# Writing out the loop over pairs of heads in a two-layer cross-attention kernel

## The reference, cut to what matters

```python
# layer 0: 8 heads of 16; layer 1: 16 heads of 32, with layer norms ahead of its projections
Qh, Kh, Vh = split(Q @ W_q), split(K @ W_k), split(V @ W_v)
scores = jnp.einsum('bqhd,bkhd->bhqk', Qh, Kh) * scale      # 4096 x 3202 for each head
attn = jax.nn.softmax(scores, axis=-1)
ctx = jnp.einsum('bhqk,bkhd->bqhd', attn, Vh).reshape(b, lq, H * DV)
X = Q + ctx @ W_o
...
# layer 0: relu(X @ w1.T + b1) @ w2.T + b2 + X; layer 1: the same with silu and 2048 hidden
```

## Time and profile before

| | |
|---|---|
| median of 3 runs | 5738.86 us (5737.87 to 5742.69) |
| the profiled execution | 5741.43 us |
| its span in the trace | 5739.7 us |
| instructions in the trace | 103849 |
| TensorE matmuls busy | 5364.3 us, 93% of the span |
| VectorE, ScalarE, GpSimd busy | 3997.0 us (70%), 3200.2 us (56%), 2329.3 us (41%) |
| a0: its first exponential and that of a1 | 434.39 us and 2030.48 us from the span's start |

### The profile page before, as it was taken

One profiled execution on the slowest core, in us unless ns is written; L12 is line 12 of the kernel. 1 busy time (PEld: TensorE's weight loads), 2 busy tenths in 40 slices (PEclk: granted clock), 3 DMA queues, 4 the chain that ended last, 5 costly groups with the idle time before them and its releaser, 6 DMA issues. The chain is left out here.

```text
span 5739.7 us, 103849 instructions
## 1 busy us (share of the span) xinstructions
PE 5364.3 (93%) x28676; PEld 3368.1 (59%) x28676; DVE 3997.0 (70%) x6906; ACT 3200.2 (56%) x5849; POOL 2329.3 (41%) x1156
## 2 busy tenths in 40 slices
PE   5959999999979799999999999999999998899999
PEld 4834444444447565655565656555565664677777
DVE  4439888888847688888787878878788886332231
ACT  3317777777733256666666666666666665222222
POOL 0000000000000068888787888878788887000000
PEclk9969999999979899999999999999999999899999
DMA  3451111111144321111111111111111111322220
GB/s 99 125 132 30 37 37 37 37 36 37 28 140 120 108 66 41 39 41 28 40 39 42 39 29 39 41 39 40 28 39 41 41 28 44 111 96 81 81 88 22
DMA packets 328588, 325.61 MB, mean 57 GB/s; under 512 B 184624, under 2 KB 192688, under 8 KB 326064
## 3 DMA queue, kind: packets, MB, share of 16 engines
q1 hardware_dynamic: 328112, 319.92, 21.0%
HBM read 219.18 MB, written 100.53 MB: 56 GB/s over the span
## 5 line engine op out<-in xcount | busy, mean ns | idle before, releaser
L777 DVE TENSOR_REDUCE a_maxes<-a_mscore 128x1 f32<-128x458 f32 (+4 forms) x5376 | 3039.4, 625 | 668.7 <-PE a_mscore L836 640.3
L760 ACT ACTIVATE a_prob<-a_score 128x512 f32<-128x512 f32 x4992 | 2633.6, 598 | 1271.2 <-PE a_score L845 1260.6
L845 PE MATMUL a_score<-a_q,a_k 97*128 97x512 f32 (+1 forms) x4992 | 1993.4, 434 | 54.3 <-DMA a_q<-row 31.6
L836 PE MATMUL a_mscore<-a_k,a_qm 96*128 96x458 f32 (+4 forms) x5376 | 1901.1, 417 | 69.8 <-DMA a_k<-k 56.0
L864 PE MATMUL a_acc<-a_prob,a_v 128*32 128x512 f32 x9984 | 1613.0, 608 | 0.0
L836 PEld LDWEIGHTS a_mscore<-a_k,a_qm 96*128 96x128 f32 (+1 forms) x5376 | 1479.1, 310 | 192.1 <-issue 71.9
L726 POOL TENSOR_TENSOR a_added<-a_added,a_prob 128x1024 f32<-128x1024 f32 x640 | 1527.8, 2387 | 55.5 <-POOL a_added L726 0.2
L845 PEld LDWEIGHTS a_score<-a_q,a_k 97*128 97x128 f32 (+1 forms) x4992 | 924.8, 195 | 1028.1 <-ACT a_prob L760 534.9
L723 POOL TENSOR_TENSOR a_added<-a_prob 128x1024 f32<-128x1024 f32 x128 | 305.3, 2385 | 2053.7 <-ACT a_prob L760 2043.3
L859 PE MATMUL a_acc<-a_prob,a_ones 128*1 128x512 f32 x2048 | 965.1, 593 | 0.0
L864 PEld LDWEIGHTS a_acc<-a_prob,a_v 128*32 128x32 f32 x9984 | 293.4, 109 | 304.4 <-issue 155.7
(11 more groups left out here) (188 smaller groups left out, 3905.9 us busy)
## 6 DMA issues: line engine op xcount, KB each, us to landing
a_qm<-q SPq DMA_DIRECT2D x384, 64.0 KB, 1.8
a_q<-q SPq DMA_DIRECT2D x384, 64.0 KB, 1.8
acc<-a_acc_sb SPq DMA_DIRECT2D x384, 64.0 KB
e_part<-acc SPq DMA_DIRECT2D x90, 256.0 KB, 3.4
a_k<-k SPq DMA_DIRECT2D x48, 416.0 KB, 5.8
q<-m_qout SPq DMA_DIRECT2D x128, 128.0 KB, 2.3
e_wo<-wo_split SPq DMA_DIRECT2D x32, 512.0 KB, 4.1
k<-kv_out SPq DMA_DIRECT2D x30, 512.0 KB, 2.7
```

Source lines behind the costliest of these rows:

```text
L760: act.activation(prob[:, t], score[SCORES[it.j][t]][:], ACT.Exp, scale=SCALE).then_inc(exp_done, 1)
L777: dve.tensor_reduce(maxes[j][:, t, c:c + 1], mscore[u % UNIT_BANKS][:, 0:wide], AX.X, ALU.max).then_inc(unit_read, 1)
L836: pe.matmul(mscore[u % UNIT_BANKS][:, 0:wide], qm[j][r:r + ROW, t:NB:NB // P], kt[kk][r:r + ROW, at:at + wide], start=True, stop=True).the ...
L845: pe.matmul(score[SCORES[it.j][t]][:], kt[it.k][r:r + C, i * P:(i + 1) * P], qt[it.j][r:r + C, :], start=True, stop=True).then_inc(score_d ...
```

## The change

In `items`, the three-part form (first pair, `Fori` over the middle pairs, last pair) becomes a Python loop over all pairs. The inner `Fori` of each head stays. The items, their order, the transfers and the semaphores are the same; the pair's number is now a constant everywhere.

```diff
-            yield from pair(0, True, False)
-            with eng.Fori(1, PAIRS - 1) as p:
-                yield from pair(p, False, False)
-            yield from pair(PAIRS - 1, False, True)
+            for p in range(PAIRS):
+                yield from pair(p, p == 0, p == PAIRS - 1)
```

## The result

The changed kernel takes **5678.35 us** (median of 4 runs, 5676.18 to 5686.56), the kernel before 5738.98: a ratio of 0.9896, 95% interval 0.9879 to 0.9913, 60.6 us less. Forecast were 5685 us and 54.2 us less. Four more runs of the same kernel later had a median of 5684.57, which is 54.6 us under the 5739.15 of the kernel before beside them. The profiled execution took 5679.2 us around a span of 5677.4.

What follows compares the result with a forecast made beforehand. TensorE, busy 93% of the span, was taken as the bound, starved of code when the middle loop branches back. Savings of 44.7 and 9.5 us, together 54.2, gave 5685 us (0.94% less), range 5679 to 5699.

Steps and rivals of the forecast that it cites:

- The back edges of a1: Sixteen-head attention, middle loop: its five branches back are removed, all on the path, saving 38.1 us.
- The back edge of a0: Eight-head attention, middle loop: its one branch back is removed, saving 5.0 us.
- The remainder, put to SyncE's register work: Sixteen-head attention's middle heads: 6.6 us beyond the back edges, put to SyncE's register work and ends of inner loops.
- rival A: Middle loops: only the back edges go, the remainder stays; gain 42 us, time 5697; chance 0.10.
- no stretch of low clock between the first and the last head: Long attention, changed profile: sign of a right forecast, no low-clock stretch between those heads.
- More code at no cost: Both attentions: twelve heads' worth of code becomes twenty-four, costed at nothing.
- Rival B: Inner loops' new copies begin to miss, 7.4 us each on TensorE; chance 0.04 for one to three, 0.03 for nine or more.
- Rival C: Pair starts: the stall belongs to the place, only eight branches of 0.1 us go, time 5738; chance 0.02.
- The profiled execution took 5741.43 us around a span of 5739.7; it becomes 5687.2: Whole kernel: 54.2 us taken off the profiled execution; span becomes 5685.5, median of the runs 5685.
- the sum of 54.2 us: Middle heads of both attentions: 44.7 us saved in the sixteen-head one plus 9.5 in the eight-head one.

Runs made afterwards that it cites:

- two_trips: Kernel before with the long attention's middle loop as two trips of three written-out pairs, the short attention's loop kept: 5706.92 us, ratio 0.9941.
- all_but_pe: Kernel before with the middle loop written out for the four other engines and kept in TensorE's program alone: 5725.81 us, ratio 0.9968.
- pe_only: Kernel before with the middle loop written out in TensorE's program alone, kept by the other four engines: 5692.74 us, ratio 0.9916.
- pe_and_sp: Kernel before with the middle loop written out for TensorE and SyncE, kept by ScalarE, VectorE and GpSimd: 5681.08 us, ratio 0.9897.
- kv_late_looped: Kernel before, middle loop kept, with SyncE's loads of the next head's keys and values behind the row of maxima: 5705.05 us, ratio 0.9938.
- kv_late: Changed kernel with SyncE's loads of the next head's keys and values moved behind the row of maxima: 5652.78 us, ratio 0.9841.
- one_trip: Against the kernel before, each middle pair in a single-trip loop of its own, whose branch never goes back: 5680.48 us, ratio 0.9896.
- after_again: The changed kernel run and profiled once more, nothing altered: 5684.57 us, ratio 0.9897 to the kernel before.
- after: The changed kernel in its first series, middle loop over pairs written out against the kernel before: 5678.35 us, ratio 0.9896.
- warm_end: Changed kernel with one added product for each of the 26 score tiles of an attention's last item: 5692.06 us, ratio 0.9913.
- best: Changed kernel with key and value loads behind the row of maxima and added products in the last items: 5647.27 us, ratio 0.9843.

## Why the prediction was right, and where it was off

- **The back edges of a1**: forecast 38.1 us, measured 38.3 at the same five boundaries. That the branch back is the cause is shown by two_trips (one branch back, one boundary at 52.5 us) and by all_but_pe (TensorE's loop alone keeps all five). That the time goes to fetching code rests on the packets of queue q8, which follow TensorE's loop alone (218 with it and 189 without; the earlier trace rows, pe_only and all_but_pe), and on the length of what is jumped over: in a1 TensorE's branch back is cheap in the inner loop, at most 233 ns with a body of some 610 instructions in the trace, and dear in the middle loop, 3.3 to 4.2 us with a body of some 3700. With a body three times as long (two_trips) the branch takes 4.5 us and the boundary 52.5 us, little more than the 50.7 to 52.2 of before. No run put a shorter body at this place, so at what length it becomes dear is open.
- **The back edge of a0**: forecast 5.0; the boundary went from 61.0 to 56.5, 4.5 us. All four heads gained 7.9 us in the first profile and 9.8 in the second, where 9.5 were forecast. That it is TensorE's branch alone isn't shown: all_but_pe, which keeps it, has heads 2 to 5 at 576.6 us, like the changed kernel.
- **The remainder, put to SyncE's register work**: forecast 6.6 us in a1. two_trips gives 5 to 9, and pe_and_sp against pe_only shows that SyncE carries 9.3 us when it keeps its loop, registers and branch together. kv_late_looped against kv_late adds that it is gone when the row no longer comes behind the loads. The attribution holds; rival A, that it would stay, fell. In the first profile 2.7 us of it are missing, since one head's start was late (46.5 us for the first two items of head 5, with 3.4 us at the low clock). So one sign named beforehand, no stretch of low clock between the first and the last head, did not come there. The second profile has none and the whole forecast, 2128.2 - 2083.5 = 44.7.
- **More code at no cost**: right. In straight code TensorE is busy for 173.3 of 173.6 us a head, and less code was fetched in all (189 packets against 218 on q8).
- **Rival B, inner loops that miss**: no passage over 223 ns at 24 places. (Its chances name one to three misses and nine or more, and leave out four to eight.) **Rival C, the place**: the places are there, the stall is not. The 0.1 us a branch that this rival reckons with is near what one_trip's branches take that don't go back (67 to 76 ns on TensorE); before, the middle loop's branches took 3.3 to 4.2 us there when they went back.
- **What put the median outside the range** is the step "The profiled execution took 5741.43 us around a span of 5739.7; it becomes 5687.2". It carried the profiled execution's clock in a0's last item over to the median of the changed kernel. With the low clock there, as in after_again, the forecast of the span was 5685.5 and the trace says 5687.4; without it the time is 10.7 us lower. By their times that happened in three of the four runs of the first series (one of them was profiled and shows it). So for the change itself the sum of 54.2 us came out as 51.6 to 52.3, and the 60.6 us of the medians are partly luck. The row was in the trace before (28.3 us, clock 0.50) and I hadn't read it; the range should have reached 11 us further down.

## What to carry to other kernels

Where a loop's branch has a median of microseconds on the engine that sets the time (3.6 us here), while shorter loops' branches on the same engine take a few hundredths of that (0.15 us), write the long loop out (on that engine, and on the queue that feeds it) and keep the short ones. On the other engines look for the stall behind the branch, at the next register instruction (2.4 to 3.9 us later here). Forecast it by the neighbours: if the first and last trips are already written out, their rows give the price of the rest. And before a small difference is given to a change, look for stretches outside it whose clock differs between the two profiles.

## What the runs showed of the hardware that was not expected

- Time at a low clock adds half as much again to the idle time: TensorE stood idle for 2.33 and 2.64 us, and from 0.9 us behind the first of these stretches on the granted clock was 0.50 for 6.8 us. By an estimate from these rows, some 4.6 us of the 6.8 are not inside the second idle stretch and lose about half, 2.3 us, which makes 7.3 with the idle time. By the windows a branch back is 7.7 us (38.3 over five) and not 5.
- Behind a branch back of 50 ns on SyncE and ScalarE the next register instruction comes 2.6 and 3.4 us later. Only on TensorE does the branch itself show the stall (3.3 to 4.2 us; 45 to 63 ns on the other four).
- An item with few matmuls takes 17.6 or 28.3 us in different executions of one program (after and after_again), at granted clocks of 1.00 or 0.50, and 26 more matmuls in it went with 0.52 in one profile (warm_end) and 1.00 in another (best).
- A loop of a single trip still runs its branch (34 to 40 ns on SyncE) but no longer has register work beyond its counter's (3254 ALU_OPs on ScalarE, 3246 without the loop, 5318 before).
